# Adding expert tiles by indirect transfers into rows that already hold residual and shared expert

## The reference, cut to what matters

```
logits = x @ router_w.T                      # x: normalised residual, 2048 tokens x 256
top_vals, top_idx = top_k(logits, 2);  gates = sigmoid(top_vals)
h   = silu(gate) * up                        # gate, up = split(x @ gate_up_w[e])
moe = sum over the two chosen experts e of  gates[e] * (h @ down_w[e])
shared = (silu(x @ shared_gate_w.T) * (x @ shared_up_w.T)) @ shared_down_w.T
out = residual + moe + shared
```

## Time and profile before

| | us |
|---|---|
| median of 3 runs (range) | 1454.44 (1449.91 to 1455.63) |
| the profiled execution, its own time | 1457.18 |
| span in its trace | 1455.5 |
| loop over tiles: first scatter issued, last one issued | 1290.2, 1429.0 |
| from the last scatter's landing to the end | 24.4 |

### The profile page before, as it was taken

How to read it: one execution, slowest core, us unless ns; L and a number is a source line. 1 busy time by engine, 2 the same in 40 slices (tenths; PEclk the granted TensorE clock), 3 DMA queues, 4 the chain that set the end, 5 groups by cost and what they waited for, 6 DMA issues and landing times. The chain is left out here.

```text
span 1455.5 us, 17983 instructions
## 1 busy us (share of the span) xinstructions
PE 1262.4 (87%) x5610; PEld 563.5 (39%) x5610; DVE 921.5 (63%) x2110; ACT 670.5 (46%) x1245; POOL 498.5 (34%) x734
## 2 busy tenths in 40 slices
PE   4798989878898889998998998998789889999992
PEld 2232332322243224453443443443242335566661
DVE  4798878888988786566566566568557523233334
ACT  2255445555555555555445455455446551112220
POOL 5433251153302411326226225225213122236651
PEclk9699999989999899999999999999999999999996
DMA  7842322413430333113123113124513005612225
GB/s 237 233 131 80 125 72 73 115 48 117 132 114 24 102 88 96 51 59 102 45 59 102 45 59 102 44 60 118 122 52 82 1 30 152 226 43 82 82 57 173
DMA packets 113007, 135.83 MB, mean 93 GB/s; under 512 B 15745, under 2 KB 92037, under 8 KB 112659
## 3 DMA queue, kind: packets, MB, share of 16 engines
q1 hardware_dynamic: 105075, 122.01, 29.1%
q0 software_dynamic: 5664, 10.57, 2.4%
q10 hardware_dynamic: 2176, 2.10, 0.5%
HBM read 87.57 MB, written 48.53 MB: 94 GB/s over the span
## 5 line engine op out<-in xcount | busy, mean ns | idle before, releaser
L1252 DVE TENSOR_REDUCE Mx<-bank 128x1 f32<-128x512 f32 x512 | 340.9, 685 | 249.0 <-PE bank L994 247.2
L890 ACT ACTIVATE prob<-bank 128x512 f32<-128x512 f32 x544 | 314.9, 596 | 289.1 <-PE bank L1020 287.7
L994 PE MATMUL bank<-KS,QS 96*128 96x512 bf16 x768 | 303.7, 397 | 49.3 <-DVE Mx L1249 19.6
L1020 PE MATMUL bank<-QS,KS 99*128 99x512 bf16 x768 | 298.9, 390 | 47.1 <-DVE prob L1263 19.6
L890 ACT ACTIVATE prob<-prob 128x512 f32<-128x512 f32 x224 | 141.1, 630 | 170.4 <-DVE prob L1263 169.2
L1033 PE MATMUL bank<-prob,V 128*17 128x512 f32 x1536 | 212.4, 626 | 0.7 <-ACT prob L890 0.7
L1020 PEld LDWEIGHTS bank<-QS,KS 99*128 99x128 bf16 x768 | 75.1, 98 | 264.4 <-ACT prob L890 107.8
L994 PEld LDWEIGHTS bank<-KS,QS 96*128 96x128 bf16 x768 | 76.1, 99 | 192.3 <-DVE Mx L1249 63.1
L735 POOL TENSOR_SCALAR MR<-neg 16x128 bf16<-16x128 f32 x48 | 13.8, 288 | 266.9 <-ACT neg L865 266.6
L1249 DVE CUSTOM_DVE_ANT_0 bank<-bank,mask 128x512 f32<-128x512 f32 x128 | 87.6, 696 | 22.2 <-PE bank L994 21.7
L1249 DVE CUSTOM_DVE_ANT_0 bank<-bank,ff_h 128x512 f32<-128x512 f32 x128 | 88.0, 694 | 20.0 <-PE bank L994 19.6
(11 more groups left out here) (176 smaller groups left out, 1803.6 us busy)
## 6 DMA issues: line engine op xcount, KB each, us to landing
stack_scr<-parts SPq DMA_DIRECT2D x48, 384.0 KB, 2.6
QS<-stack_scr SPq DMA_DIRECT2D x48, 384.0 KB, 4.2
KS<-stack_scr SPq DMA_DIRECT2D x48, 384.0 KB, 5.1
stack_scr<-parts SPq DMA_DIRECT2D x48, 256.0 KB, 2.9
w_gu<-in_gate_up SPq DMA_DIRECT2D x16, 512.0 KB, 9.7
stack_scr<-parts SPq DMA_DIRECT2D x48, 128.0 KB, 2.8
cT<-in_ctxT SPq DMA_DIRECT2D x8, 512.0 KB, 5.7
w_dn<-in_down SPq DMA_DIRECT2D x16, 256.0 KB, 9.3
```

Source lines behind the costliest of these rows:

```text
L890: act.activation(prob[:, u % NP_, j, :], src, ACT.Exp, scale=CAST).then_inc(exp_done, 1)
L994: pe.matmul(bankS[i % NS][:, :], QS[0:STACK, h, qt * P:(qt + 1) * P], KS[0:STACK, h, :], start=True, stop=True).then_inc(s_full, 1)
L1020: pe.matmul(bankT[e % NT][:, :], KS[0:ROWS, h, kt * P:(kt + 1) * P], QS[0:ROWS, h, :], start=not on_pe, stop=True).then_inc(t_full, 1)
L1252: dve.tensor_reduce(dst, b, AX.X, ALU.max).then_inc(s_read, 1)
```

## The change

`y_tok` is gone. A new array `sums` in the main memory has one row for each token and 128 spare ones. SP stores `acc` (residual and shared expert) there as soon as each batch has it. Every tile's scatter adds its rows to `sums` (`compute_op=ALU.add`) in place of writing them. As a token is in two tiles and an addition reads the row and writes it back, each scatter waits until the one before it has landed: `sum_out`, one semaphore for all. `yt` has four buffers (`NY`) in place of two. Blanks now go to the spare rows, each partition to its own, and are no longer left out. At the end SP and ACT copy `sums` to `out`, from main memory to main memory, in four transfers of 512 KB. The adding back on DVE is gone.

```
-    y_tok = nc.dram_tensor("y_tok", [2 * SLOTS, D], F32, kind="Internal").ap()
+    sums = nc.dram_tensor("sums", [SLOTS + P, D], F32, kind="Internal").ap()
...
-                pool.iota(tags[:, :, :, 0], [[P, TT], [SLOTS, 2]], base=0, channel_multiplier=1,
+                pool.iota(tags[:, :, :, 0], [[P, TT], [0, 2]], base=0, channel_multiplier=1,
...
-        got = sb("got", [P, NR, 2, D], F32)
+        nobody = sb("nobody", [P, 1], F32)
...
-        yt = sb("yt", [P, 2, D], F32)
+        yt = sb("yt", [P, NY, D], F32)
...
+        PARTS = 4
+        whole = sums[0:SLOTS].rearrange("(i r c) n -> i r (c n)", i=PARTS, r=P)
+        result = out.rearrange("b s n -> (b s) n").rearrange("(i r c) n -> i r (c n)", i=PARTS, r=P)
...  (SP)
-                for t in range(0, TT, 2):
-                    if t >= NR:
-                        sp.wait_ge(added, t - NR + 1)
-                    sp.dma_start(got[:, t % NR, :, :], y[t]).then_inc(got_in[t % NR], 16)
-                    if t >= NR:
-                        store(t - NR)
...
+                sp.dma_start(sums[SLOTS:SLOTS + P], acc[:, 0, :]).then_inc(rows_out, 16)
+                o = sums[0:SLOTS].rearrange("(b t p) n -> b p t n", b=B, p=P)
+                for b in range(B):
+                    if b >= EARLY_SHARED:
+                        sp.wait_ge(y_read, (b - EARLY_SHARED + 1) * QT)
+                    sp.dma_start(o[b], acc[:, b * QT:(b + 1) * QT, :]).then_inc(rows_out, 16)
+                sp.wait_ge(sum_out, 16 * TILES)
+                for i in range(0, PARTS, 2):
+                    sp.dma_start(result[i], whole[i]).then_inc(stored, 16)
...  (POOL)
+                pool.wait_ge(rows_out, 16 * (B + 1))
                 for s in range(TILES):
                     pool.wait_ge(yt_read, s + 1)
-                    if s >= 2:
-                        pool.wait_ge(yt_out[s % 2], 16 * (s // 2))
-                    pool.indirect_dma_start(y_tok, bass.IndirectOffsetOnAxis(home[:, s:s + 1], 0),
-                                            yt[:, s % 2, :], None, bounds_check=2 * SLOTS - 1,
-                                            oob_is_err=False).then_inc(yt_out[s % 2], 16)
+                    if s:
+                        pool.wait_ge(sum_out, 16 * s)
+                    pool.indirect_dma_start(sums, bass.IndirectOffsetOnAxis(home[:, s:s + 1], 0),
+                                            yt[:, s % NY, :], None, compute_op=ALU.add).then_inc(sum_out, 16)
...  (ACT)
-                        if n >= 2:
-                            act.wait_ge(yt_out[n % 2], 16 * (n // 2))
+                        if n >= NY:
+                            act.wait_ge(sum_out, 16 * (n - NY + 1))
...
+                act.wait_ge(sum_out, 16 * TILES)
+                for i in range(1, PARTS, 2):
+                    act.dma_start(result[i], whole[i]).then_inc(stored, 16)
...  (DVE)
+                    dve.tensor_scalar(nobody[:, :], iota_p[:, :], float(SLOTS), None, ALU.add)
...
+                    dve.tensor_scalar(home[:, :], tag[:, :], nobody[:, 0:1], None, ALU.min)
+                    dve.tensor_scalar(token[:, :], tag[:, :], SLOTS - 1.0, None, ALU.min).then_inc(token_ready, 1)
...
-                for t in range(TT):
-                    dve.wait_ge(got_in[t % NR], 16 * (t // NR + 1))
-                    for k, s in enumerate((first, added)):
-                        dve.tensor_tensor(acc[:, t, :], got[:, t % NR, k, :], acc[:, t, :], ALU.add).then_inc(s, 1)
```

More of the change, by code:

```diff
@@ L1404, in _, with experts @@
                         dve.tensor_copy(slot[:, p * QT:(p + 1) * QT, :], slotf[:, :, :]).then_inc(route_ready[p], 1)
-    experts(nc, cnt, identf, acc, tags, slot, hT_last, s_gu, s_dn, swish, tagged, t_scr, tag_scr, y_tok,
+    experts(nc, cnt, identf, acc, tags, slot, hT_last, s_gu, s_dn, swish, tagged, t_scr, tag_scr, sums,
             gate_up, down, out)
-def experts(nc, cnt, identf, acc, tags, slot, hT_last, s_gu, s_dn, sg, tagged, t_scr, tag_scr, y_tok,
+def experts(nc, cnt, identf, acc, tags, slot, hT_last, s_gu, s_dn, sg, tagged, t_scr, tag_scr, sums,
             gate_up, down, out):
@@ L1420, in experts @@
         NX = 8
-        NR = 4
+        NY = 4
         LATE = B - EARLY_SHARED
@@ L1442, in experts @@
         gate = sb("gate", [P, TILES], F32)
-        second = sb("second", [P, TILES], F32)
         home = sb("home", [P, TILES], U32)
@@ L1475, in experts @@
         yt_read = sem("yt_read")
[L1476 to L1479, removed]
+        rows_out = sem("rows_out")
+        sum_out = sem("sum_out")
         stored = sem("stored")
@@ L1483, in experts @@
         table_of = tag_scr.rearrange("(r q) c -> r (q c)", q=P)
-        y = y_tok.rearrange("(k t p) n -> t p k n", p=P, k=2)
+        PARTS = 4
+        whole = sums[0:SLOTS].rearrange("(i r c) n -> i r (c n)", i=PARTS, r=P)
+        result = out.rearrange("b s n -> (b s) n").rearrange("(i r c) n -> i r (c n)", i=PARTS, r=P)
         with nc.Block() as block:
@@ L1492, in _ @@
                     sp.dma_start(w_dn[:, n, :, :], down[n].rearrange("(k p) n -> p k n", p=P)).then_inc(w_in, 16)
[L1494 to L1500, removed]
-                for t in range(0, TT, 2):
-                    if t >= NR:
-                        sp.wait_ge(added, t - NR + 1)
-                    sp.dma_start(got[:, t % NR, :, :], y[t]).then_inc(got_in[t % NR], 16)
-                    if t >= NR:
-                        store(t - NR)
-                for t in range(TT - NR, TT, 2):
-                    store(t)
-                sp.wait_ge(stored, 8 * TT)
+                sp.dma_start(sums[SLOTS:SLOTS + P], acc[:, 0, :]).then_inc(rows_out, 16)
[7 more added lines that the diff above has]
+                    sp.dma_start(result[i], whole[i]).then_inc(stored, 16)
+                sp.wait_ge(stored, 16 * PARTS)
             @block.gpsimd
@@ L1564, in _ @@
                         act.wait_ge(yt_full, n + 1)
-                        if n >= 2:
-                            act.wait_ge(yt_out[n % 2], 16 * (n // 2))
-                        act.activation(yt[:, n % 2, :], bank[6 + n % 2][:, 0:D], ACT.Identity,
+                        if n >= NY:
+                            act.wait_ge(sum_out, 16 * (n - NY + 1))
+                        act.activation(yt[:, n % NY, :], bank[6 + n % 2][:, 0:D], ACT.Identity,
                                        scale=gate[:, n:n + 1]).then_inc(yt_read, 1)
[L1569 to L1574, removed]
+                act.wait_ge(sum_out, 16 * TILES)
+                for i in range(1, PARTS, 2):
+                    act.dma_start(result[i], whole[i]).then_inc(stored, 16)
             @block.tensor
@@ L1756, in _ @@
                                     bank[4 + s % 2][:, 0:EH]).then_inc(hT_read, 1)
-                for t in range(TT):
-                    dve.wait_ge(got_in[t % NR], 16 * (t // NR + 1))
-                    for k, s in enumerate((first, added)):
-                        dve.tensor_tensor(acc[:, t, :], got[:, t % NR, k, :], acc[:, t, :], ALU.add).then_inc(s, 1)
-                        if k == 0:
-                            dve.wait_ge(first, t + 1)
 def kernel(**inputs):
```

## The result

The changed kernel takes **1520.9 us** (median of 4 runs, 1519.5 to 1523.3) against 1455.0 for the kernel before (also 4 runs): ratio 1.046, 95% interval 1.044 to 1.048. It is slower by 66 us; 1502 was forecast, with a range of 1450 to 1600.

The account below looks back on a forecast made before the run. The loop before was taken as PE-bound at 3.02 us a tile. First scatter at 1290.18, 47 intervals of 4.25 (199.8), landing 3.5 and end 9.6 gave span 1503.0, adjusted to a 1502 us median; range 1450 to 1600.

Parts of the forecast that it names:

- The chain of landings: Tile loop: each scatter waits for the previous landing, so a tile costs 4.25 us against 3.02; chance 0.61.
- The reaction w: POOL in the tile loop: time from a landing to the start of the waiting scatter, taken as 0.75 us.
- The landing L: Adding scatter, issue to landing: 3.5 us, from a gather's 2.8, 0.3 for writing and 0.4 for the second operand.
- the things that would prove me wrong: Signs in the later profile: distance staying 3.02, scatter's instruction much over 1.02 us, or end copies taking 20 us.
- The Trainium skill's rule: Adding scatter's landing: two source reads, about half a copy's rate, giving 2.7 us; the prediction kept its higher value.
- What stands behind the waiting scatter: POOL's queue: the gather of a tile eight ahead, which PE does not yet want, so it adds nothing.
- First scatter and addresses: Before the tile loop: waiting for SP's five stores and the altered address arithmetic both cost nothing; first scatter at 1290.18.
- The end, 9.6: After the last landing: four copies 9.0 us, issue 0.1, span's remainder 0.5, in place of 24.4 us.
- The addition is not free: Answers a rival on the scatter's landing: addition costs nothing, landing 2.4, tile 3.15, kernel 1449 us; chance 0.10.
- PE does not set the pace: Answers a rival on the tile loop: landing plus reaction under 3.02 us, PE still paces, kernel near 1443; chance 0.06.
- rows one by one: Rival on landing: an engine finishes each row first, 7.7 us, kernel 1704; two at a time 4.9, 1569; chance 0.17.
- PE's clock: Rival in the tile loop: idle PE drops to half clock, 6.04 us a tile, kernel 1586; chance 0.06.

Follow-up runs that it names:

- e1: The changed kernel with its scatters writing their rows in place of adding them, waits, blanks and copies kept; ratio 1.001 to the kernel before.
- e4: The changed kernel with two arrays of sums, each scatter waiting only for the one two tiles before, odd tiles' share left out of the output; 1447.9 us, ratio 0.995.
- e11: The changed kernel with each scatter adding only the first half of each row, 512 bytes in place of 1 KB; 1503 us, ratio 1.028 to the kernel before.
- e9: The changed kernel with twelve buffers for gathered rows in place of eight; ratio 1.044 to the kernel before.
- e2: The changed kernel, still adding, with blanks left out of the transfer again; 1510.5 us, ratio 1.037 to the kernel before.
- e3: The kernel before, with each scatter to y_tok waiting for the landing of the one just before it, not two before; ratio 1.010.
- e8: The changed kernel with even tiles adding to the output, odd ones to a second array added at the end by one POOL transfer, blanks left out; ratio 0.999.
- e7: The changed kernel adding directly to the output, blanks left out and no copy at the end; ratio 1.036 to the kernel before.

## Why the prediction was right, point by point

- *The chain of landings becomes the bound.* Right, and shown by three runs that each take away one thing: the addition (e1: 3.24 us a tile), the wait for the predecessor (e4: 3.04, 3.18 in the middle, with the landing unchanged), and half of the bytes (e11: 4.13). PE's gap, POOL's waits (45, where 47 were foretold) and the even distance are in the profile. Two details did not come: ACT's `yt` waited for PE (97.4 us) and hardly for a landing (7.7 us, twice), since PE was stopped earlier, at the gathers; and PE's busy time in the phase was not unchanged but 13.6 us longer (158.6 against 145.0), for which no run gives a cause.
- *The reaction w, 0.75.* Right: from landing to the next start it is 0.77 nearly throughout, and the mean distance of 4.63 less 3.8 to 3.9 gives 0.73 to 0.83.
- *The landing L, 3.5.* The term that was mis-sized: 3.8, rising to 4.9 at times. Two sizes in it were off. The scatter's own instruction on POOL was taken as 1.02 and is 1.58; that it might grow stood among the things that would prove me wrong, not in the sum. And the part that comes with the rows was 1.1, by differences of empty and full tiles, against the 1.4 that my terms make over the empty landing of 2.1 (0.7 + 0.3 + 0.4). The errors partly cancelled, which was luck: 2.1 + 0.6 + 1.1 = 3.8. The distance came out 4.63 for 4.25, 47 times 0.38 = 18 us, and that is nearly the whole miss (1521 for 1502).
- *The Trainium skill's rule* ("Collectives: The Full Stack", Part 3: two source reads, half the rate) gave too little: what a full tile adds went from 0.3 to 1.1 us, more than twice. The Trainium skill's fit in "DMA: Bandwidth & Descriptors" (anatomy of a DMA from GpSimd: 2.0 us plus bytes over 436 GB/s) fits the plain scatter (2.4) and misses the adding one by 1.5; the page has no term for what the DMA does, which the prediction read as "whatever the operation". In its rules for kernel authors, the Trainium skill's "DMA: Bandwidth & Descriptors" says that an accumulating DMA reads its destination and writes it later, that another write of the same bytes landing in between is lost, and that the earlier DMA's semaphore has to be waited for. No run here tried it. So the wait was not taken away alone, and e4 used a second array.
- *What stands behind the waiting scatter.* "PE does not yet want it" was wrong as a statement, since PE waited 125 us for gathers, and right as a price: e9 moved these waits elsewhere for nothing.
- *First scatter and addresses: nothing.* Right: the first scatter is at 1291.2, in a phase that itself began 0.9 later.
- *The end, 9.6.* It was 8.4. Four copies from main memory to main memory land 4.2 to 7.4 us after their issue, 250 GB/s over the stretch, close to the old end's 258. So the sum in which a byte that is read and written there counts twice (16.3 us) is out. In e1 and e2 the same end took 9.3 and 8.8.
- *Rivals.* The addition is not free (e1 measures it at 65 us); PE does not set the pace; rows one by one would have meant a landing of 7.7 us, two at a time 4.9, and it was 3.8. PE's clock was granted at 1.00 of 2.4 GHz in the loop but for one fall to 1.2 GHz of 3.4 us about 1345 to 1348, with no longer distances there (4.49 and 4.60); it fell for good when PE's work was over (0.72 over 1480 to 1506).

## What to carry to other kernels

Before an update in memory replaces a write and a later read, count the loop that its ordering makes: landing plus the issuing engine's reaction (here 3.8 + 0.75), once for each dependent transfer, against what an iteration costs now (3.02). Two transfers in flight hid the same landings (e4); one in flight did not, with the transfer engines busy for 0.37 of the time. The saving at the end is paid once (16 us), the chain 47 times (79 us), so a small error in the landing decides the sign: price it from empty and full transfers of the same kind, and price the issuing instruction separately.

## What the runs showed of the hardware that I had not expected

- An adding indirect scatter takes 1.58 us of POOL's time to issue, a plain one 0.98 to 1.02. For the adding one it made no difference whether a row has 1 KB or 512 bytes (e11); with no row at all it took 1.55 (e2). With the gather's 0.98 and two gaps of 0.30 it makes POOL itself the next bound at 3.18 us (e4).
- From a landing to the start of the scatter that waited for it POOL took 0.77 us in the changed kernel, in e1 and in e9, and 0.85 in e2 and e3, whose scatters leave blanks out.
- Where POOL issued the last transfer and its landing ended the work, the span went on for 4.6 us behind it (e8 by its own landing; e7 by the 2.7 us of the scatters before it), and for about 0.5 where SP or ACT had issued it (0.4 in the changed kernel). What fills these 4.6 us no view shows, and the cause stays open.
- Adding 2.1 MB from main memory to main memory in one transfer of 8 KB pieces landed in 13.0 us, with 205 to 218 GB/s on its plateau (e8).
